# VectorE adds two pairs of products itself in the last step of each image

## The reference

```python
xdw = depthwise3x3(x) + dw_b
om = (xdw @ om_w + om_b).reshape(n, h, w, G, KK * 3)   # 9 taps: two offsets and a mask each
value = (x @ vp_w + vp_b).reshape(n, h, w, G, GC)      # 32 groups of 8 channels
sampled = bilinear corners of value at (base + tap + offset)
out = einsum('nhwgkc,nhwgk->nhwgc', sampled, mask).reshape(n, h, w, c)
x = x + out @ op_w
```

## Time and profile before

| | |
|---|---|
| time, median of 3 runs | 3767.26 us (3767.25 to 3767.76) |
| the profiled execution's own time | 3762.78 us |
| its span (first to last instruction) | 3761.0 us |
| PE busy in the span (matmul ends are modelled) | 3499.6 us (93%) |
| DVE busy | 3365.7 us (89%) |
| ACT busy | 2549.4 us (68%) |
| POOL busy | 622.6 us (17%) |
| mean granted TensorE clock | 0.989 |

### The profile page before, as it was taken

The page is one execution under the profiler, slowest core; times in us unless marked ns, Lnnn a source line. Parts: engine busy times, 40 slices in busy tenths (PEclk is TensorE's granted clock), DMA queues, the critical chain, the costliest instruction groups (busy, mean ns, idle before and its releaser), DMA issues. The chain is left out here.

```text
span 3761.0 us, 89283 instructions
## 1 busy us (share of the span) xinstructions
PE 3499.6 (93%) x36672; PEld 2250.2 (60%) x36672; DVE 3365.7 (89%) x2555; ACT 2549.4 (68%) x4937; POOL 622.6 (17%) x476
## 2 busy tenths in 40 slices
PE   4899999999999999999999999999999999858998
PEld 2566666666666666666666666666666666623333
DVE  4799899999999899989998999999998999948776
ACT  5677677777776677667776777777766666345554
POOL 0011111101111111111111111011111111104444
PEclk9999999999999999999999999999999999979999
DMA  6566676666666666667666766666666665436553
GB/s 176 123 139 123 136 158 151 131 134 145 146 139 134 126 149 142 131 132 153 149 128 136 157 143 134 139 138 146 141 130 120 129 129 101 86 151 225 210 209 147
DMA packets 329155, 537.40 MB, mean 143 GB/s; under 512 B 38268, under 2 KB 243708, under 8 KB 314760
## 3 DMA queue, kind: packets, MB, share of 16 engines
q0 software_dynamic: 103296, 263.22, 38.1%
q1 hardware_dynamic: 224584, 266.07, 24.1%
q10 hardware_dynamic: 832, 2.10, 0.2%
HBM read 262.53 MB, written 67.41 MB: 88 GB/s over the span
## 5 line engine op out<-in xcount | busy, mean ns | idle before, releaser
L1104 DVE TENSOR_TENSOR pv<-val,wsum 128x2048 f32<-128x2048 f32 x800 | 1809.0, 2284 | 139.0 <-PE ps_add L864 122.2
L864 PEld LDWEIGHTS ps_add<-ident,pv 128*128 128x128 f32 x11776 | 1282.4, 141 | 293.7 <-issue 205.3
L864 PE MATMUL ps_add<-ident,pv 128*128 128x128 f32 x11776 | 1390.8, 275 | 36.2 <-DVE pv L1104 33.9
L816 PE MATMUL ps_om<-xdw,omw 128*32 128x256 f32 x13824 | 868.0, 384 | 97.9 <-ACT hat L615 96.7
L816 PEld LDWEIGHTS ps_om<-xdw,omw 128*32 128x32 f32 x13824 | 391.2, 109 | 418.6 <-ACT hat L615 146.8
L613 ACT ACTIVATE hat<-ps_om,omb 128x256 f32<-128x256 f32 x576 | 275.1, 478 | 394.7 <-PE ps_om L816 375.1
L1043 DVE TENSOR_TENSOR prod<-hat,mwy 128x1536 f32<-128x1536 f32 (+1 forms) x272 | 347.7, 1312 | 43.8 <-DMA wsum<-prod 33.1
L787 PE MATMUL ps_bg<-tri,diag 128*32 128x512 f32 x3024 | 345.8, 591 | 12.1 <-ACT tri L579 12.1
L568 ACT ACTIVATE tri<-tri,gn_tri 96x1024 f32<-96x1024 f32 (+1 forms) x376 | 329.8, 949 | 4.7 <-ACT gn_tri L536 4.4
L1029 DVE TENSOR_TENSOR mwy<-hat,msk 128x768 f32<-128x768 f32 x288 | 273.6, 950 | 55.3 <-ACT hat L627 55.3
L489 POOL DMA_DIRECT2D wsum<-acc x80 | 98.8, 1235 | 1248.7 <-DVE wsum L1043 1248.7
(11 more groups left out here) (153 smaller groups left out, 3256.0 us busy)
## 6 DMA issues: line engine op xcount, KB each, us to landing
tri<-in_x_dram SPq DMA_DIRECT2D x725, 128.0 KB, 3.3
pv<-pv POOLq DMA_DIRECT2D x64, 1024.0 KB, 7.6
wsum<-acc POOLq DMA_DIRECT2D x80, 768.0 KB, 7.3
wsum<-prod POOLq DMA_DIRECT2D x80, 768.0 KB, 7.5
win<-in_x_dram SPq DMA_DIRECT2D x144, 256.0 KB, 3.5
x<-xres SPq DMA_DIRECT2D x128, 256.0 KB, 2.9
xres<-in_x_dram POOLq DMA_DIRECT2D x124, 256.0 KB, 11.0
out_dram<-c_x SPq DMA_DIRECT2D x31, 1024.0 KB, 4.3
```

The lines of the kernel that those rows point to most:

```text
L816: mm = nc.tensor.matmul(ps_om[G * q:G * q + G, (par + i) % 2, 0:TOK], omw[:, h, comp, :], xdw[:, j % 2, h, q, :], start=h == 0, stop=h == ...
L864: mm = nc.tensor.matmul(ps_add[:, tb, c, :], pv[:, (j + uv) % PBUF, c, P * tb:P * tb + P], consts["ident"][:, :], start=uv == ADDED[0] and ...
L1104: nc.vector.tensor_tensor(pv[:, (j + uv) % PBUF, :, :].rearrange("p c (r w) -> p c r w", w=W), val[:, :, SR * j + u:SR * j + u + SR, v:v + ...
```

## The change

In step j = 3 of each image (`heavy`) two more pairs are formed: product 4 goes into 5, and 7 into 8. VectorE does it itself, with an in-place addition of 128 x 2048 directly behind the multiplication that makes 5 (or 8), and waits for that multiplication first. TensorE's list in that step loses 4 and 7, which were the early ones of parts 6 and 7; 5 and 8 wait for a new semaphore and stand in the late place. The waits for free buffers and the counts of sums follow. The other steps are as they were.

```diff
+HEAVY_PAIRED = {5: 4, 8: 7}
-ADDED = [uv for k in (4, 5, 6, 7, 8, 0, 1, 2, 3) for uv in ADDS_AT[k]]
+HEAVY_ADDS_AT = ADDS_AT[:6] + [(3, 5, 6), (8, 9)] + ADDS_AT[8:]
+def heavy(j):
+    return j % STEPS == STEPS - 1
+def paired(j):
+    return {**PAIRED, **HEAVY_PAIRED} if heavy(j) else PAIRED
+def adds_at(j, k):
+    return (HEAVY_ADDS_AT if heavy(j) else ADDS_AT)[k]
...
-                def add(s, j, uv):
+                def add(n, j, uv):
+                    s, order = STEPS * n + j, added(j)
                     if uv in PAIRED:
-                        pe.wait_ge(pair_added, 16 * (len(PAIRS) * s + PAIRS.index(uv) + 1))
+                        pe.wait_ge(pair_added, 16 * (pairs_before(n, j, uv) + 1))
+                    elif uv in paired(j):
+                        pe.wait_ge(pair_made, len(HEAVY_PAIRED) * n + sorted(HEAVY_PAIRED).index(uv) + 1)
                     else:
                         pe.wait_ge(pv_full, SHIFTS * s + uv + 1)
...
-                        before = [uv for uv in ADDS_AT[k][:1] if uv not in PAIRED]
+                        before = [uv for uv in adds_at(j, k)[:1] if uv not in paired(j)]
...
                                             val[:, :, SR * j + u:SR * j + u + SR, v:v + W], w_in, ALU.mult)\
                         .then_inc(pv_full, 1)
+                    if heavy(j) and uv in HEAVY_PAIRED:
+                        dve.wait_ge(pv_full, SHIFTS * s + uv + 1)
+                        total = pv[:, (j + uv) % PBUF, :, :]
+                        nc.vector.tensor_tensor(total, total, pv[:, (j + HEAVY_PAIRED[uv]) % PBUF, :, :], ALU.add)\
+                            .then_inc(pair_made, 1)
```

More of the change, by code:

```diff
@@ L40 @@
 PAIRED = {1: 0, 3: 2}
-PAIRS = list(PAIRED)
+HEAVY_PAIRED = {5: 4, 8: 7}
 ADDS_AT = [(13, 14, 15), (16, 17, 18), (19, 20, 21), (22, 23, 24), (), (1,), (4, 3, 5, 6), (7, 8, 9), (10, 11, 12)]
-ADDED = [uv for k in (4, 5, 6, 7, 8, 0, 1, 2, 3) for uv in ADDS_AT[k]]
-ADDS = len(ADDED)
+HEAVY_ADDS_AT = ADDS_AT[:6] + [(3, 5, 6), (8, 9)] + ADDS_AT[8:]
 SENT_TAPS = (1, 2, 3, 6, 7)
@@ L70, in following, with added, pairs_before, adds_before @@
     return (n, j + 1) if j < STEPS - 1 else (n + 1, 0)
+def heavy(j):
[4 more added lines that the diff above has]
+    return (HEAVY_ADDS_AT if heavy(j) else ADDS_AT)[k]
+def added(j):
+    return [uv for k in (4, 5, 6, 7, 8, 0, 1, 2, 3) for uv in adds_at(j, k)]
+def pairs_before(n, j, uv):
+    return len(PAIRED) * (STEPS * n + j) + sorted(PAIRED).index(uv)
+def adds_before(n, j):
+    return n * sum(len(added(i)) for i in range(STEPS)) + sum(len(added(i)) for i in range(j))
 def previous(n, j):
@@ L274, in layer0 @@
         pv_full, add_done, add_out = sem("pv_full"), sem("add_done"), sem("add_out")
-        pair_added = sem("pair_added")
+        pair_added, pair_made = sem("pair_added"), sem("pair_made")
         xres_added, stats2 = sem("xres_added"), sem("stats2")
@@ L495, in add_pair @@
                     pool.wait_ge(pv_full, SHIFTS * s + uv + 1)
-                    at_least(pool, pair_added, 16 * (len(PAIRS) * s + PAIRS.index(uv)))
-                    nc.gpsimd.dma_start(pv[:, (j + uv) % PBUF, :, :], pv[:, (j + PAIRED[uv]) % PBUF, :, :],
+                    at_least(pool, pair_added, 16 * pairs_before(n, j, uv))
+                    nc.gpsimd.dma_start(pv[:, (j + uv) % PBUF, :, :], pv[:, (j + paired(j)[uv]) % PBUF, :, :],
                                         accum_op=ALU.add).then_inc(pair_added, 16)
@@ L628, in hats, with summed @@
                                          scale=-1.0).then_inc(hat_full, 1)
-                def summed(s):
-                    act.wait_ge(add_done, ADDS * (s + 1))
+                def summed(n, j):
+                    act.wait_ge(add_done, adds_before(*following(n, j)))
                     for tb in range(TB):
@@ L726, in step @@
                             act.wait_ge(wsum_added, 16 * (sent_before(TAPS) * s + sent_before(4)))
-                            summed(s - 1)
+                            summed(*previous(n, j))
                         if k + 2 < TAPS:
@@ L765, in _ @@
                 statistics(NI - 1, STEPS - 2, (0, 1))
-                summed(STEPS * NI - 1)
+                summed(NI - 1, STEPS - 1)
                 at = unit(NI - 1, STEPS - 1, "project3", NI) + 1
@@ L852, in group_mean @@
                                      start=True, stop=True).then_inc(bg_full, 2)
-                def add(s, j, uv):
+                def add(n, j, uv):
+                    s, order = STEPS * n + j, added(j)
                     if uv in PAIRED:
-                        pe.wait_ge(pair_added, 16 * (len(PAIRS) * s + PAIRS.index(uv) + 1))
+                        pe.wait_ge(pair_added, 16 * (pairs_before(n, j, uv) + 1))
+                    elif uv in paired(j):
+                        pe.wait_ge(pair_made, len(HEAVY_PAIRED) * n + sorted(HEAVY_PAIRED).index(uv) + 1)
                     else:
                         pe.wait_ge(pv_full, SHIFTS * s + uv + 1)
-                    if uv == ADDED[0]:
+                    if uv == order[0]:
                         at_least(pe, add_out, s)
@@ L864, in add @@
                             mm = nc.tensor.matmul(ps_add[:, tb, c, :], pv[:, (j + uv) % PBUF, c, P * tb:P * tb + P],
-                                                  consts["ident"][:, :], start=uv == ADDED[0] and c % 4 == 0,
-                                                  stop=uv == ADDED[-1], is_transpose=True, skip_group_check=True)
+                                                  consts["ident"][:, :], start=uv == order[0] and c % 4 == 0,
+                                                  stop=uv == order[-1], is_transpose=True, skip_group_check=True)
                     mm.then_inc(add_done, 1)
@@ L886, in add_next @@
                     def add_next(k, early):
-                        before = [uv for uv in ADDS_AT[k][:1] if uv not in PAIRED]
-                        for uv in before if early else ADDS_AT[k][len(before):]:
+                        before = [uv for uv in adds_at(j, k)[:1] if uv not in paired(j)]
+                        for uv in before if early else adds_at(j, k)[len(before):]:
                             if k >= SAMPLED:
-                                add(s, j, uv)
+                                add(n, j, uv)
                             elif not first:
-                                add(s - 1, j - 1, uv)
+                                add(*previous(n, j), uv)
                     def place(name):
@@ L932, in _ @@
                 for k in range(SAMPLED):
-                    for uv in ADDS_AT[k]:
-                        add(STEPS * NI - 1, STEPS - 1, uv)
+                    for uv in adds_at(STEPS - 1, k):
+                        add(NI - 1, STEPS - 1, uv)
                 at = unit(NI - 1, STEPS - 1, "project3", NI) + 1
@@ L1096, in multiply @@
                         dve.wait_ge(wadd_done, (TAPS - 1 - len(SENT_TAPS)) * s + kept_before(k + 1))
[L1097 to L1101, removed]
+                    used, of = (uv - PBUF, (n, j)) if uv >= PBUF else (uv - PBUF + SHIFTS, previous(n, j))
+                    into = {v: k for k, v in paired(of[1]).items()}
+                    if used in into and into[used] in PAIRED:
+                        dve.wait_ge(pair_added, 16 * (pairs_before(*of, into[used]) + 1))
+                    elif used in into:
+                        dve.wait_ge(pair_made, len(HEAVY_PAIRED) * of[0] + sorted(HEAVY_PAIRED).index(into[used]) + 1)
+                    elif uv >= PBUF or not is_step(n, j, 0, 0):
+                        dve.wait_ge(add_done, adds_before(*of) + added(of[1]).index(used) + 1)
                     w_in = wsum[:, u, v, :].rearrange("p (r w) -> p r w", w=W).unsqueeze(1)\
```

## The result

The changed kernel takes 3754.07 us (median of 7 runs, 3753.33 to 3757.01), the kernel before 3767.31 in the same comparison (3765.71 to 3772.41): a ratio of 0.9963, 95% interval 0.9952 to 0.9974. On another occasion it was 0.9967 (0.9956 to 0.9978). That is 13 us or 0.35% faster; 10.8 us were forecast. The two profiled executions lie 8.7 us apart (3762.78 and 3754.04).

A forecast was written before the change was run, and what follows sets the result against it. The bound was taken to alternate between TensorE and VectorE. Winning 5 x 2.3 + 1.5 + 2.0 = 15.0 us and losing 4.25 in the last step gives -10.8: 3767.26 to 3756.5 us, range 3748 to 3768 (own range 3753 to 3761).

The forecast's parts named there:

- TensorE saves 1.36 us a sum: Parts 6 and 7 of step 3: each removed early sum saves 1.36 us, not 1.89, as TensorE waits for ScalarE.
- VectorE pays 2.44 us an addition: Step 3: each in-place addition costs 2.20 us plus 0.24 for waiting on its own product; two cost 4.88.
- the last step: End of image 7: additions lie on the path, 4.88 less a 0.63 us wait, so 4.25 us lost.
- Through step 3: Product 7's 3.04 us wait goes, it starts 0.60 us earlier; VectorE leaves step 3 1.84 us later, TensorE 2.72 earlier.
- Through step 0 to product 7: Sum 13 waits 0.65 us for its product; TensorE stays 2.4 us ahead, VectorE's lateness is hidden by product 7.
- The rival in which VectorE's lateness carries over: TensorE, held at sum 13, keeps VectorE's pace in step 0; 1.84 us added per image, 17.1 lost, 3784 us; chance 0.11.
- the one in which TensorE saves the full sums: ScalarE ready and product 13 in time: 3.78 us saved per image, 22 won, 3745 us; chance 0.07.
- The DMA in between: Step 0, part 6's wsum DMA, needed by part 7's product: nearly all is kept, 2.3 us for each of five images.
- The rival's mechanism: Step 0: part 6's DMA lands late, VectorE regains only 0.8 us an image, 3766 us; with no gain 3771.5; chance 0.27.
- The single images: Gains by image: 2.3 us in five, 1.5 in image 2 for its 12.0 us DMA, 2.0 in image 6.
- The prediction's own sign of being wrong: Step 0: TensorE's sums 14 to 24 wait for products, or VectorE waits for the DMA more than 2 us.
- Steps 1 and 2 as they were: Steps 1 and 2 of each image keep their length; VectorE was said to hardly wait there.

The follow-up runs named there:

- experiment 1: Kernel before, with VectorE making products 5 and 8 of each image's last step twice, the second behind a wait for the first; TensorE's sums unchanged: 3770.84 us, ratio 1.001.
- experiment 2: Changed kernel without VectorE's additions, so products 4 and 7 are missing from the sums of step 3: 3741.49 us, ratio 0.9931.
- Experiment 9: Changed kernel, last image's products of parts 6 and 8 in steps 0 and 1 put into buffer acc instead of prod: 3751.74 us, ratio 0.9957.
- experiment 5: Kernel before, with the 1 MB load ahead of step 0 cut to 128 of 2048 columns in images 1 to 6: 3766.88 us, ratio 1.0001.
- experiment 10: Changed kernel, with the change left out in the last image and both early places of step 3 filled with sums again: 3752.39 us, ratio 0.9961.
- experiment 12: Kernel before, unchanged, run again for a second profile: 3764.45 us.
- experiment 6: Changed kernel, with the 1 MB load ahead of step 0 cut to 128 of 2048 columns in images 1 to 6: 3755.37 us, ratio 0.9972.

## Why the prediction was right

TensorE's saving, VectorE's price and the way to product 7 of step 0 are right in mechanism and size. The closeness of the total, 13 against 10.8, is in part luck: the images keep 9.5 us where 15.0 were forecast, step 1 adds 4.7 that were put at nothing, and some 3 us lie outside the steps.

- *TensorE saves 1.36 us a sum.* Right. Without the sum the third component starts 1635.96 - 1633.57 = 2.39 us behind the first, with 0.46 of waiting; 2.40 was taken from part 5.
- *VectorE pays 2.44 us an addition.* 0.11 too much. The addition lasts 2.29 us; from product 5 to the addition it is 1636.00 - 1633.67 = 2.33, from there to product 6 2.21, of which 2.21 would have been there anyway: 2.33 more. It lies between the 2.20 and the 2.44 of the two readings: waiting for its own result costs VectorE 0.12 us here, and as much in experiment 1. The Trainium skill ("VectorE: DVE Perf Modes", section "The DRAIN you can't avoid") says that the semaphore costs nothing extra; the trace disagrees, by that 0.12 us. In the last step that is 2 x 2.33 - 0.63 = 4.0 us, and 3.9 was measured, not 4.25.
- *Through step 3.* Product 7 starts 1643.02 - 1633.67 = 9.35 us behind product 5 instead of 10.14: 0.8 earlier (forecast 0.6). The step's end is 1.5 later (forecast 1.84).
- *Through step 0 to product 7.* Sum 13 waits for its product for 0.65 us, as worked out, and product 7 is 2.4 us earlier (forecast 2.3, and 2.4 ahead of the DMA's share). Experiment 1 shows that VectorE's share is hidden up to there, experiment 2 that TensorE's alone gives the same interval. The rival in which VectorE's lateness carries over is refuted by both, the one in which TensorE saves the full sums by the 0.46 us.
- *The DMA in between.* This is the term that was mis-sized. The wait ahead of the product of part 7 came, and as worked out it is covered by the wait for TensorE at product 7. But I stopped there. The DMA of part 7 had been just in time for the product of part 8, too, and it leaves only when the product of part 7 is made: relative to product 5 of step 3 that product stands at 1742.33 - 1636.67 = 105.66 before and 1738.96 - 1633.67 = 105.29 after the earlier trace rows, 0.4 us earlier, and 0.7 in the mean of seven images. The product of part 8 can gain on that only what its DMA had to spare: it waits 1.15 us, and comes 1.3 us earlier than before, in this image and in the mean, not 2.4. So an image keeps 1.4 us, not 2.3, by the end of step 0: 9.5 us over seven, where 15.0 were forecast. Experiment 9 shows this cause in image 7 by taking it away, experiment 2 in all seven by letting VectorE come on time. The rival's mechanism was therefore partly at work, one part later than I had placed it.
- *The single images.* Image 2 was to gain least for its slow DMA, and gained most: 2.2 us. Its 12.0 us were one execution's; after the change that DMA took 8.9. Images 1, 3, 4, 5 and 7 gained 1.1 to 1.5, image 6 0.6.
- *The prediction's own sign of being wrong.* It named a wait for the DMA of more than 2 us. The single waits in step 0 reach 2.01 at most, but the waits for DMAs of one step 0 sum to 2.7 to 3.7 us in images 1 and 3 to 6. By the sum the sign had come, and it did point at the term that was off.
- *Steps 1 and 2 as they were.* Wrong for step 1: 4.7 us less, nearly all of it in images 5 to 7 (1.4, 2.4, 1.2), where before has longer waits for `wsum` DMAs. The reading behind it was wrong as well: VectorE does wait in steps 1 before the change, 27.0 us for DMAs in all, nearly always ahead of the same two products of parts 7 and 8. Part 8 of image 6, before and after:

```profile
2657.29 2.36 DVE L1043 TENSOR_TENSOR prod<-hat,mwy 128x1536 f32<-128x1536 f32 x2 [3.10 <-DMA wsum<-prod]
```
```profile
2646.98 2.36 DVE L1075 TENSOR_TENSOR prod<-hat,mwy 128x1536 f32<-128x1536 f32 x2 [1.19 <-DMA wsum<-prod]
```

  Both profiles of before have these long steps (image 6: 100.4), both of after the short ones (98.0 and 97.9), so it isn't chance. The gain comes with TensorE's share: experiment 2 has it (787.5 us), experiment 1 nearly none of it (791.9). Why only in those images, no run tells. Together with the 3.9 of the last step the two errors cancel in part: -9.5 - 4.7 + 0.2 + 3.9 = -10.1 for the steps, against -10.8.
- *The median.* It fell by 12.7 to 13.2 us, the sum of the profiled steps by 7.7 to 10.1 between the two profiles of before and the two of after. The remainder of 2.6 to 5.5 us is open; the clock behind the last step can be a part of it, if the two kernels don't meet it equally often, which was not counted.

## What to carry to other kernels

In these steps VectorE had less to do than TensorE, and the work given to it cost nothing as far as its waits for TensorE reached. Such a wait has to be looked for at the very place: by the medians the same addition was worth 5.8 us ahead of a 3 us wait and 1.0 behind it. Where an operation only fills the time until another engine has emptied a bank, taking it away saves less than it lasts (1.36 of 1.89 us). And when an engine starts earlier, follow each buffer that it writes through its DMA to the *next* user and the one behind that; here a transfer that had been just in time became late, and the one behind it in the same buffer handed on what the first had lost. A row of one trace can be one execution's: what rests on a single image's wait wants a second profile.

## What the runs showed of the hardware

Behind the last step, 16 matmuls of 128 x 512 take 7.13 us in ten of the 14 profiled executions and 9.29 to 9.46 in the other four (experiments 2, 5, 10 and 12); before and experiment 12 are the same kernel. In experiment 5, of the second kind, the granted clock of that stretch is 0.77, in before 1.00 (stretch, busy PE, PEld, DVE, ACT, POOL, clock, DMA; before, then experiment 5):

```profile
3295.00:3302.30 7.30, 7.13 (x16) 2.96 (x16) 2.07 (x3) 2.57 (x5) 0.00 (x0) 1.00 0.00 0
```
```profile
3296.00:3305.40 9.40, 9.29 (x16) 3.75 (x16) 2.11 (x4) 2.48 (x4) 0.00 (x0) 0.77 0.00 0
```

TensorE had gone at VectorE's pace for some 30 us by then, with 0.24 us idle ahead of each sum, and had then stood for 2.09 us waiting for ScalarE. It had done the same in the first kind, so what decides between the two is not shown. A mean of 0.77 lies between the levels of 2.4 and 1.2 GHz. Counted from the last step's end, the group is done 2.9 us later (52.76 us in experiment 12, 49.85 in before), of which 0.6 stand in the transposes ahead of it.

The accumulating DMA of part 6 (768 KB from `prod` into `wsum`) in step 0 landed after 8.6 to 12.0 us before, and after 8.9 to 9.7 with the change. With the load ahead of it cut, it took 8.5 to 10.0 us in images 1 to 6 of experiment 5, where before has 10.3 to 12.0, and 8.8 to 9.8 in experiment 6, where after has 8.9 to 9.7. So the load costs it 0.6 to 3.2 us before the change and 0.9 at most after it; the 8.5 us that are always left are the larger part of what the kernel meets.
